# Weights and tables loaded inside the layer norms of a two-block network, not in stages of their own

## Chip, core and metric

One NeuronCore of one Trainium2 chip. The metric is the device time of one execution in microseconds, the median of the runs; every other time here comes from one profiled execution.

## What is computed

The input x is (4, 1024, 128) in float32: T = 4096 tokens of 128 channels. Two blocks follow one another, each of the form `x = x + s * silu(g)` with `xn = layernorm(x)`, where s is an attention of xn and g a small network of xn:

```python
xn = _layernorm(x); s = _L0_attn_ref(xn, ...)          # tiled softmax attention
g = _silu(_L0_ffn_ref(xn, ...))                        # layernorm*w+b, convolution, rotary causal attention,
x = x + s * g                                          #   layernorm*w+b, mixture of 4 experts
xn = _layernorm(x); s = _L1_attn_ref(xn, ...)          # causal attention, 16 heads
g = _silu(_L1_ffn_ref(xn, ...))                        # 6 layers: shift, local attention, shift,
x = x + s * g                                          #   layernorm*g+b, gated network
```

`_layernorm` is `(x - mean) / sqrt(var + 1e-5)` over the 128 channels, in some places followed by a weight and a bias.

## The kernel before

Activations lie transposed in SBUF, 128 channels on the partitions and 4096 tokens along the free dimension, 16 KB a partition: `x`, `s` and `cur` live through the whole program. The work is cut into stages (class `Stage`, L53), each a block of hand-written programs for the five engines with semaphores between them. At the end of a stage all engines meet in a barrier that also clears the stage's semaphores (the helper behind it has line L65 in the profile), and the next stage reuses them. Nothing of a stage starts before all engines are through with the one before. Inside a stage each engine runs its instructions in the order in which they are written.

`build_program` (L1518) writes the stages one after the other: load; ln0 (x to cur); tile attention in a loop over the 4 batches; load; ln1; convolution; the projections ci0; causal attention; load; ln2; router; experts; load; ln3; ci1; causal attention; load; and a loop over the 6 layers with shift1, local attention, shift2, ln4 and the gated network; then the end stage, which stores the output in 8 pieces. The change deals with the first four of the five load stages.

Of the kernel before, what the change touches and what calls it, by code (L numbers as in the profile page):

```python
# [105 lines left out]
def load_constants(nc, pairs):  # L106

    with Stage(nc, "load") as st:
        loaded = st.sem("loaded")
        with nc.Block() as block:  # L110

            @block.sync
            def _(sp):
                for dst, src in pairs:
                    sp.dma_start(dst, src).then_inc(loaded, 16)  # L115
                sp.wait_ge(loaded, 16 * len(pairs))

def layernorm(nc, name, ps, k, src, dst, weight=None, bias=None, fetches=()):  # L119

    with Stage(nc, name) as st:
# [6 lines left out]
        with nc.Block() as block:  # L130
# [27 lines left out]
            @block.scalar  # L158
            def _(act):
                for c in range(NCH):  # L160
                    act.wait_ge(centred, c + 1)
                    if c >= 4:
                        act.wait_ge(var_part, c - 3)
                    nc.scalar.activation(square[:, c % 4, :], dst[:, chunk(c)], ACT.Square).then_inc(squared, 1)  # L164
                act.wait_ge(var_eps, 1)
                nc.scalar.activation(rstd[:, :], rstd[:, :], ACT.Sqrt).then_inc(rooted, 1)  # L166
                if weight is not None:
                    for c in range(NCH):
                        act.wait_ge(scaled, c + 1)
                        nc.scalar.activation(dst[:, chunk(c)], dst[:, chunk(c)], ACT.Identity,  # L170
                                             bias=bias, scale=weight).then_inc(done, 1)
                    act.wait_ge(done, NCH)
# [1345 lines left out]
def build_program(nc, a, out):  # L1518

    with ExitStack() as whole:
# [12 lines left out]
        with ExitStack() as before:  # L1534
            k = dict(k, **buffers(before, CAUSAL))
            with ExitStack() as ctx:
                w = buffers(ctx, [n for n in a if n.startswith("ta_") and n != "ta_bv"])
                w["ta_bv"] = ctx.enter_context(nc.sbuf_tensor("sb_ta_bv", [P, P], F32))
                load_constants(nc, loads(k) + [(x[:, :], a["x"])] +
                               [(t[:], a[n].to_broadcast([P, P]) if n == "ta_bv" else a[n]) for n, t in w.items()])  # L1540
                layernorm(nc, "ln0", ps, k, x, cur)
                tile_attention(nc, ps, k, w, cur, s)

            with ExitStack() as ctx:
                vtok = ctx.enter_context(nc.sbuf_tensor("vtok0", [P, NT, P], F32))
                stacks, zeros = causal_stacks(nc, ctx, "ca0")
                w = buffers(ctx, ["cq", "ck", "cv", "cqs", "cks", "cproj", "taps", "ln1"])
                with ExitStack() as inner:
                    h, mixed = (inner.enter_context(nc.sbuf_tensor(n, [P, T], F32)) for n in ("h0", "h_mixed"))  # L1550
                    tables = buffers(inner, ["cos", "sin"])
                    load_constants(nc, loads(w) + loads(tables))
                    layernorm(nc, "ln1", ps, k, cur, h, w["ln1"][:, 0:1], w["ln1"][:, 1:2])
                    causal_convolution(nc, w["taps"], h, mixed)
                    causal_inputs(nc, "ci0", ps, mixed, dict(q=w["cq"], k=w["ck"], v=w["cv"], q_swapped=w["cqs"],
                                                             k_swapped=w["cks"]), tables, q_parts, k_parts, vtok, stacks, zeros)
                causal_attention(nc, "ca0", ps, k, q_parts, k_parts, vtok, stacks, zeros, w["cproj"], cur, cur)
            with ExitStack() as ctx:
                h = ctx.enter_context(nc.sbuf_tensor("h1", [P, T], F32))
                mask = ctx.enter_context(nc.sbuf_tensor("mask", [P, NT, E], BF16))  # L1560
                w = buffers(ctx, ["wv", "wp", "router", "ln2"])
                load_constants(nc, loads(w))
                layernorm(nc, "ln2", ps, k, cur, h, w["ln2"][:, 0:1], w["ln2"][:, 1:2])
                route(nc, ps, w["router"], h, mask)
                experts(nc, ps, k, w["wv"], w["wp"], h, mask, cur, s, x)

            with ExitStack() as ctx:
                vtok = ctx.enter_context(nc.sbuf_tensor("vtok1", [P, NT, P], F32))
                stacks, zeros = causal_stacks(nc, ctx, "ca1")  # L1570
                w = buffers(ctx, ["dq", "dk", "dv", "dproj"])
                load_constants(nc, loads(w))
                layernorm(nc, "ln3", ps, k, x, cur)
                causal_inputs(nc, "ci1", ps, cur, dict(q=w["dq"], k=w["dk"], v=w["dv"]), None, q_parts, k_parts, vtok, stacks, zeros)
                causal_attention(nc, "ca1", ps, k, q_parts, k_parts, vtok, stacks, zeros, w["dproj"], s, None)

# [152 lines left out]
```

## Time and profile before

| | us |
|---|---|
| median of 3 runs | 5986.9 (5984.35 to 5988.27) |
| the profiled execution | 5988.87 |
| its span in the trace | 5987.1 |
| PE busy | 4994.9 (83%) |
| DVE busy | 3999.0 (67%) |
| ACT busy | 3194.9 (53%) |
| POOL busy | 1770.2 (30%) |

The mean granted TensorE clock is 0.939 of full. A matmul, activation or vector instruction is told with the instant at which it starts, how long it ran, and in brackets how long its engine was idle before it and what released it; `SPq` rows are SP issuing a DMA. "PEq L65" as a releaser is the barrier between stages.

### The profile page before, as it was taken

The page shows a single profiled execution, that of the slowest core. Times are in us where ns is not written, and L with a number is a line of the kernel's source. Part 1 is how long each engine was busy: PE and PEld are TensorE (multiplying, and loading weights), DVE is VectorE, ACT ScalarE, POOL GpSimd, SP SyncE. Part 2 cuts the span into 40 slices and gives each one's busy share as a digit, 9 for nine tenths or more (in the row PEclk, how much of TensorE's full clock was granted, in tenths as well). Part 3 has the DMA queues.
Part 4 walks back from the last instruction along what each step waited for, and adds up shares of the span by engine and source line. Part 5 has one row for each costly group of instructions (what it writes and reads, how often), then busy time and mean ns, then how long its engine had stood idle before and what let it go on. Part 6 is the DMA issues. An engine that isn't in the chain of part 4 may idle for free. (4 is left out here: it accounts for less than half of the span.)

```text
span 5987.1 us, 168239 instructions
## 1 busy us (share of the span) xinstructions
PE 4994.9 (83%) x74422; PEld 2903.2 (48%) x74640; DVE 3999.0 (67%) x4814; ACT 3194.9 (53%) x3632; POOL 1770.2 (30%) x1242
## 2 busy tenths in 40 slices
PE   6757888688678877998899889987999799979997
PEld 3432333343333334665466546663666366636663
DVE  5767775332477756886688658865887488848884
ACT  2324556122245554775477546763776377636773
POOL 0020000000200004552355325542555155505550
PEclk9988999899889998999999999998999899989998
DMA  0011000000110001111111101110111111101111
GB/s 25 0 48 34 27 25 13 21 0 0 50 29 23 23 13 53 38 38 41 27 37 39 45 22 35 38 52 16 38 38 34 33 38 38 38 30 38 38 38 40
DMA packets 90446, 187.28 MB, mean 31 GB/s; under 512 B 26112, under 2 KB 42368, under 8 KB 87552
## 3 DMA queue, kind: packets, MB, share of 16 engines
q1 hardware_dynamic: 89728, 176.58, 11.3%
q8 instruction: 588, 9.63, 0.7%
q14 instruction: 130, 1.06, 0.1%
HBM read 60.10 MB, written 14.68 MB: 12 GB/s over the span
## 5 line engine op out<-in xcount | busy, mean ns | idle before, releaser
L1413 POOL TENSOR_TENSOR part_of_local<-part_of_local,sine_of_local 128x512 f32<-128x512 f32 x768 | 960.9, 1273 | 1060.7 <-DVE sine_of_local L1350 1060.7
L820 ACT ACTIVATE prob_of_ca<-ps 128x1024 f32<-128x1024 f32 (+3 forms) x768 | 600.0, 812 | 414.3 <-PE ps L667 254.7
L1420 POOL TENSOR_TENSOR part_of_local<-part_of_local,inverse_of_local 128x1024 f32<-128x1024 f32 x384 | 722.6, 1903 | 142.9 <-DVE inverse_of_local L1382 142.9
L685 PE MATMUL ps<-keys_of_ca,queries_of_ca 64*128 64x512 bf16 (+3 forms) x1536 | 329.5, 350 | 244.0 <-DVE top_of_ca L858 97.8
L1387 DVE TENSOR_REDUCE total_of_local<-prob_of_local 128x16 f32<-128x1024 f32 x192 | 234.3, 1220 | 417.0 <-ACT prob_of_local L1326 417.0
L1347 DVE TENSOR_TENSOR part_of_local<-ps,rope 128x1024 f32<-128x1024 f32 x384 | 466.4, 1215 | 45.0 <-ACT square_of_local L1294 45.0
L1186 PE MATMUL ps<-qkv,shifted 128*128 128x512 f32 x768 | 395.9, 639 | 88.9 <-POOL values_of_local L1423 77.5
L1350 DVE TENSOR_TENSOR sine_of_local<-ps,rope 128x1024 f32<-128x1024 f32 x384 | 465.9, 1213 | 0.0
L1196 PE MATMUL ps<-qkv,shifted 128*128 128x512 f32 x768 | 381.6, 619 | 82.6 <-ACT heads_out_of_local L1322 68.8
L1272 PEld LDWEIGHTS ps<-prob_t_of_local,mixed_of_local 64*64 64x64 f32 x12288 | 338.3, 134 | 165.0 <-issue 154.9
L858 DVE TENSOR_REDUCE top_of_ca<-ps 128x2 f32<-128x1024 f32 (+1 forms) x320 | 356.6, 1114 | 82.0 <-PE ps L667 64.5
L1281 PE MATMUL ps<-heads_out_of_local,wo 128*128 128x128 f32 x3072 | 392.5, 283 | 14.3 <-ACT heads_out_of_local L1322 14.1
L1272 PE MATMUL ps<-prob_t_of_local,mixed_of_local 64*64 64x32 f32 x12288 | 386.0, 220 | 14.8 <-issue 7.9
L1272 PE MATMUL ps<-prob_t_of_local,values_of_local 64*64 64x32 f32 x12288 | 381.9, 219 | 0.8 <-issue 0.2
L1281 PEld LDWEIGHTS ps<-heads_out_of_local,wo 128*128 128x128 f32 x3072 | 374.5, 199 | 16.4 <-ACT heads_out_of_local L1322 16.4
L1253 PE MATMUL ps<-qkv,shifted 128*64 128x512 f32 x1536 | 372.9, 606 | 0.0
L1312 ACT ACTIVATE keys_of_local<-ps 128x1024 f32<-128x1024 f32 x192 | 196.8, 1025 | 324.7 <-PE ps L1215 324.7
L1333 ACT ACTIVATE values_of_local<-ps 128x1024 f32<-128x1024 f32 x192 | 196.6, 1024 | 302.9 <-PE ps L1253 302.9
L1272 PEld LDWEIGHTS ps<-prob_t_of_local,values_of_local 64*64 64x64 f32 x12288 | 339.0, 135 | 2.5 <-issue 1.9
L759 PE MATMUL ps<-prob_of_ca,values_of_ca 128*32 128x512 f32 (+3 forms) x3072 | 335.8, 510 | 0.6 <-ACT summed_of_ca L806 0.4
L852 DVE TENSOR_REDUCE top_of_ca<-ps 128x1 f32<-128x512 f32 x384 | 262.9, 685 | 97.2 <-PE ps L685 96.8
L636 POOL COPY values_of_ca<-vtok 128x256 f32<-128x256 f32 x32 | 12.8, 402 | 1035.2 <-PE ps L759 1035.1
(206 smaller groups left out, 10169.1 us busy)
## 6 DMA issues: line engine op xcount, KB each, us to landing
mixed_of_local<-values_of_local SPq DMA_DIRECT2D x636, 128.0 KB
mixed_of_local<-values_of_local SPq DMA_DIRECT2D x264, 64.0 KB
queries_of_ca<-q_parts SPq DMA_DIRECT2D x384, 32.0 KB
keys_of_ca<-k_parts SPq DMA_DIRECT2D x384, 32.0 KB
qkv<-in_qkv SPq DMA_DIRECT2D x7, 1536.0 KB, 6.6
rope<-in_rope SPq DMA_DIRECT2D x7, 1024.0 KB, 9.1
q_parts<-parts_of_ci SPq DMA_DIRECT2D x16, 384.0 KB, 2.5
k_parts<-parts_of_ci SPq DMA_DIRECT2D x16, 384.0 KB, 2.5
```

What stands on the lines that cost most here:

```text
L759: last = nc.tensor.matmul(ps[h * QUAD:(h + 1) * QUAD, SUM_BANK, j:], values[:, G % 2, kt, h, :], prob[:, i % 2, h, j:], start=kt == 0, sto ...
L820: nc.scalar.activation(prob[:, i % 2, 2 * two:2 * two + 2, j:], ps[:, 2 * two:2 * two + 2, j:], ACT.Exp, scale=scale).then_inc(raised, 1)
L858: nc.vector.reduce_max(to, pair[:, :, 0:width], AX_X).then_inc(pair_used, 1)
L1186: last = nc.tensor.matmul(two_banks(SCORE_SLOT)[:, a, :], xs[:, tokens(t)], w["qkv"][:, 0, chunk(a)], start=True, stop=True)
L1196: last = nc.tensor.matmul(two_banks(KEY_SLOT)[:, a, :], xs[:, tokens(t)], w["qkv"][:, 1, chunk(a)], start=True, stop=True)
L1253: last = nc.tensor.matmul(two_banks(VALUE_SLOT)[h * DH:(h + 1) * DH, a, :], xs[:, t * P + a * DH:t * P + (a + 1) * DH], w["qkv"][:, 2, chu ...
L1272: last = nc.tensor.matmul(out, src[rows, t % RING * 2 + i // 2, p + e, :], prob_t[rows, p + e, i * WIN:(i + 1) * WIN], start=True, stop=True)
L1281: last = nc.tensor.matmul(two_banks(OUT_SLOT)[:, 0, 0:P], w["o"][:, p, :], heads_out[:, p, :], start=p == 0, stop=p == PAIRS - 1)
L1347: nc.vector.tensor_tensor(part[:, t % 2, side], by_head(slot), table(2 * side, t), ALU.mult).then_inc(parts, 1)
L1350: nc.vector.tensor_tensor(sine[:, side], by_head(slot), table(2 * side + 1, t), ALU.mult).then_inc(parts, 1)
L1413: nc.gpsimd.tensor_tensor(out, out, sine[:, side, :, (1 - to) * half:(2 - to) * half], ALU.add).then_inc(rotated, 1)
L1420: nc.gpsimd.tensor_tensor(part[:, t % 2, side], part[:, t % 2, side], by, ALU.mult).then_inc(scaled, 1)
```

## The change

1. The three `load_constants` ahead of ln1, ln2 and ln3 are dropped, and their loads become `fetches` of these layer norms. The fifth load stage stays.
2. The first load stage loads only x, now in 8 pieces of 512 tokens and ahead of the others, and the three constants that a layer norm uses (`mean`, `mean_row`, `pick_row`). The other constants and the weights of tile attention are `fetches` of ln0.
3. A flag `late_weight`, set for ln1 and ln2, whose own weight and bias (`w["ln1"]`, `w["ln2"]`) are among the fetches: ACT waits for all fetches after the root and before the first scaling.

```diff
-def layernorm(nc, name, ps, k, src, dst, weight=None, bias=None, fetches=()):
+def layernorm(nc, name, ps, k, src, dst, weight=None, bias=None, fetches=(), late_weight=False):
...
                 nc.scalar.activation(rstd[:, :], rstd[:, :], ACT.Sqrt).then_inc(rooted, 1)
+                if late_weight:
+                    act.wait_ge(fetched, 16 * len(fetches))
                 if weight is not None:
...
-                load_constants(nc, loads(k) + [(x[:, :], a["x"])] +
-                               [(t[:], a[n].to_broadcast([P, P]) if n == "ta_bv" else a[n]) for n, t in w.items()])
-                layernorm(nc, "ln0", ps, k, x, cur)
+                first = {n: k[n] for n in ("mean", "mean_row", "pick_row")}
+                load_constants(nc, [(x[:, chunk(c)], a["x"][:, chunk(c)]) for c in range(NCH)] + loads(first))
+                layernorm(nc, "ln0", ps, k, x, cur, fetches=loads({n: t for n, t in k.items() if n not in first}) +
+                          [(t[:], a[n].to_broadcast([P, P]) if n == "ta_bv" else a[n]) for n, t in w.items()])
...
-                    load_constants(nc, loads(w) + loads(tables))
-                    layernorm(nc, "ln1", ps, k, cur, h, w["ln1"][:, 0:1], w["ln1"][:, 1:2])
+                    layernorm(nc, "ln1", ps, k, cur, h, w["ln1"][:, 0:1], w["ln1"][:, 1:2], loads(w) + loads(tables), True)
...
-                load_constants(nc, loads(w))
-                layernorm(nc, "ln2", ps, k, cur, h, w["ln2"][:, 0:1], w["ln2"][:, 1:2])
+                layernorm(nc, "ln2", ps, k, cur, h, w["ln2"][:, 0:1], w["ln2"][:, 1:2], loads(w), True)
...
-                load_constants(nc, loads(w))
-                layernorm(nc, "ln3", ps, k, x, cur)
+                layernorm(nc, "ln3", ps, k, x, cur, fetches=loads(w))
```

The order of instructions shows what this does to SP's queue. At the start of the program (L115 is the load stage, the names are buffer and DRAM tensor), the difference on SP:

```order
 L112 UNCONDITIONAL_BRANCH
-L115 DMA sb_ident<-in_ident 128x128
-L115 DMA sb_ident_b<-in_ident_b 128x128
+L115 DMA x<-in_x 128x512 x8
 L115 DMA sb_mean<-in_mean 128x128
 L115 DMA sb_mean_row<-in_mean_row 128x64
 L115 DMA sb_pick_row<-in_pick_row 128x1024
```

The eight pieces of x have moved ahead of the constants, and the two identities have left the stage (as have, below these rows, the other 16 loads; x stood among them in one piece).

On SP around ln1, before, the end of the load stage and what follows it (L132 is SP's part of the layer norm, L499 that of ci0):

```order
L115 DMA sb_cks<-in_cks 128x128
L115 DMA sb_cproj<-in_cproj 128x512
L115 DMA sb_taps<-in_taps 128x3
L115 DMA sb_ln<-in_ln 128x2
L115 DMA sb_cos<-in_cos 128x1024
L115 DMA sb_sin<-in_sin 128x1024
L110 UNCONDITIONAL_BRANCH
L132 UNCONDITIONAL_BRANCH
L499 UNCONDITIONAL_BRANCH
L505 DMA q_parts<-parts_of_ci 128x3x512
```

and after the change, from the end of the loop over batches:

```order
L199 COMPARE_AND_BRANCH
L132 UNCONDITIONAL_BRANCH
L135 DMA sb_cq<-in_cq 128x128
L135 DMA sb_ck<-in_ck 128x128
L135 DMA sb_cv<-in_cv 128x128
L135 DMA sb_cqs<-in_cqs 128x128
L135 DMA sb_cks<-in_cks 128x128
L135 DMA sb_cproj<-in_cproj 128x512
L135 DMA sb_taps<-in_taps 128x3
L135 DMA sb_ln<-in_ln 128x2
L135 DMA sb_cos<-in_cos 128x1024
L135 DMA sb_sin<-in_sin 128x1024
```

The same ten loads in the same order, now behind the entry to the layer norm (L132) and not ahead of it.

## Rows read from the trace of the kernel before

**Rows 1.** The page: span, and busy time of each engine

```profile
span 5987.1 us, 168239 instructions
PE 4994.9 (83%) x74422; PEld 2903.2 (48%) x74640; DVE 3999.0 (67%) x4814; ACT 3194.9 (53%) x3632; POOL 1770.2 (30%) x1242
```

**Rows 2.** Timeline, first loading: start us, us, engine, line, operation, out<-in, count [idle before]

```profile
0.76 0.40 SPq L115 DMA_DIRECT2D sb_ident<-in_ident  x1
...
6.42 0.43 SPq L115 DMA_DIRECT2D x<-in_x  x1
...
11.03 0.53 SPq L115 DMA_DIRECT2D sb_ta_bv<-in_ta_bv  x1
...
17.98 8.72 PE L144 MATMUL ps<-x,sb_mean 128*128 128x512 f32 x16 [17.98 <-PEq L65]
```

**Rows 3.** Timeline, second loading and ln1

```profile
332.60 0.34 SPq L115 DMA_DIRECT2D sb_cq<-in_cq  x1
...
342.88 10.10 PE L144 MATMUL ps<-cur,sb_mean 128*128 128x512 f32 x16 [12.15 <-PEq L65]
...
370.19 0.69 DVE L188 TENSOR_TENSOR h<-h,ps 128x512 f32<-128x512 f32 x1 [0.17 <-PE ps L155]
371.05 0.69 DVE L188 TENSOR_TENSOR h<-h,ps 128x512 f32<-128x512 f32 x1 [0.17 <-PE ps L155]
```

**Rows 4.** Timeline, third and fourth loading, with ln2 and the start of ln3

```profile
1078.16 0.69 DVE L905 TENSOR_TENSOR cur<-ps,cur 128x512 f32<-128x512 f32 x1 [3.91 <-PE ps L723]
1079.98 0.38 SPq L115 DMA_DIRECT2D sb_wv<-in_wv  x1
...
1091.58 9.52 PE L144 MATMUL ps<-cur,sb_mean 128*128 128x512 f32 x16 [13.45 <-PEq L65]
...
1106.22 0.63 ACT L166 ACTIVATE rstd_of_ln<-rstd_of_ln 128x512 f32<-128x512 f32 x1 [0.56 <-DVE rstd_of_ln L181]
...
1113.12 0.81 ACT L170 ACTIVATE h<-h,sb_ln 128x512 f32<-128x512 f32 x1 [6.27 <-DVE h L188]
...
1546.36 0.33 SPq L115 DMA_DIRECT2D sb_dq<-in_dq  x1
...
1551.11 10.15 PE L144 MATMUL ps<-x,sb_mean 128*128 128x512 f32 x16 [8.94 <-PEq L65]
```

**Rows 5.** Timeline, ln4 of the first layer, which has loads beside it

```profile
2796.96 10.15 PE L144 MATMUL ps<-shifted,sb_mean 128*128 128x512 f32 x16 [5.94 <-PEq L65]
2797.07 0.35 SPq L135 DMA_DIRECT2D qkv<-in_qkv  x1
...
2825.18 0.69 DVE L188 TENSOR_TENSOR normed<-normed,ps 128x512 f32<-128x512 f32 x1 [0.17 <-PE ps L155]
```

**Rows 6.** Stretches: us, busy share of each engine, granted clock, DMA share, GB/s

```profile
2797.00:2808.00 11.00, 11.00 (x24) 4.13 (x24) 5.51 (x8) 2.52 (x4) 0.00 (x0) 0.72 0.77 292
2.00:3.00 1.00, 0.00 (x0) 0.00 (x0) 0.00 (x0) 0.00 (x0) 0.00 (x0) 1.00 0.42 96
...
332.00:333.00 1.00, 0.00 (x0) 0.00 (x0) 0.00 (x0) 0.00 (x0) 0.00 (x0) 0.50 0.00 0
...
1082.00:1083.00 1.00, 0.00 (x0) 0.00 (x0) 0.00 (x0) 0.00 (x0) 0.00 (x0) 0.89 0.76 295
1084.00:1085.00 1.00, 0.00 (x0) 0.00 (x0) 0.00 (x0) 0.00 (x0) 0.00 (x0) 0.50 0.99 426
5977.00:5978.00 1.00, 0.00 (x0) 0.00 (x0) 1.00 (x2) 0.10 (x1) 0.00 (x0) 0.50 0.70 262
```

**Rows 7.** Timeline, ACT's part of the second shift in layers 1, 2 and 3

```profile
2792.47 3.62 ACT L1071 ACTIVATE shifted<-cur 64x4096 f32<-64x4096 f32 x1 [5.28 <-PEq L65]
...
3405.93 3.62 ACT L1071 ACTIVATE shifted<-cur 64x4096 f32<-64x4096 f32 x1 [3.55 <-PEq L65]
...
4023.48 3.62 ACT L1071 ACTIVATE shifted<-cur 64x4096 f32<-64x4096 f32 x1 [5.06 <-PEq L65]
```

**Rows 8.** DMA issues: out<-in, count, KB each, median us from issue to landing

```profile
sb_spread_total<-in_spread_total SPq DMA_DIRECT2D x1, 256.0 KB, 2.7
```

## Prediction, made before the changed kernel ran

> **What bounds the kernel now.** I read the page first: TensorE is busy 83% of a span of 5987.1 us and VectorE 67% [rows 1]. That average is made in the attention parts and says nothing about the places that the change touches. So I went to the timeline around each of the four loading stages. In each of them every compute engine stands still: the columns of PE, DVE and ACT are zero while the DMA columns are not [rows 6]. A loading stage is an island: the stage before has ended, SP issues loads, waits for the last to land, and only then does a barrier let the layer norm begin. Its whole length is on the path that sets the end, whatever the average says.
>
> The four lengths are read as follows. In the first, SP issues 21 loads from 0.76 us, x being the 13th at 6.42 and the last at 11.03; the first matmul of the layer norm starts at 17.98 [rows 2]. In the second, PE's last matmul ended at 330.73 (342.88 less the 12.15 of idle in its row), SP issues from 332.60, and the layer norm starts at 342.88 [rows 3]. In the third, VectorE's last sum starts at 1078.16, SP issues from 1079.98, the layer norm starts at 1091.58 [rows 4]. In the fourth SP issues from 1546.36 and the layer norm starts at 1551.11 [rows 4].
>
> The kernel also has the form that the change wants: in the loop of six layers, layer norm ln4 starts its matmuls at 2796.96 and SP issues its first load at 2797.07, with no stage between [rows 5]. Over the 11 us from 2797 the DMAs move 292 GB/s, and the engines work beside them [rows 6].
>
> **The change part by part.**
>
> *The three dropped stages (ln1, ln2, ln3).* Without the stage, the barrier behind the work before opens on the layer norm itself. SP then issues its first load at the time at which it does now, and by ln4 the first matmul starts 0.11 us before SP's first load [rows 5]. So PE starts at 332.49, 1079.87 and 1546.25 where it started at 342.88, 1091.58 and 1551.11: gains of 10.39, 11.71 and 4.86 us, **26.96 us** together. SP issues the same 10, 4 and 4 loads; they only stand in another stage, and nothing else is on SP's queue until the first store of parts, one stage or two later. What hides them is the layer norm. Its length without any load beside it: in ln1, from 342.88 to the last multiplication, which starts at 371.05, 28.17 us [rows 3]. With 3.1 MB of loads beside it, in ln4, from 2796.96 to 2825.18: 28.22 us [rows 5]. The cost of the loads to the engines is 0.05 us, which I take as nothing.
>
> *The two added waits.* ACT now waits for all loads after the square root and before the eight scalings. Behind it on ACT stand only those eight, and what waits for them is the barrier. In ln2, where most is loaded, the square root starts 14.64 us after the first matmul (1106.22 less 1091.58) and the first scaling 21.54 us after it (1113.12) [rows 4]. The loads took 11.6 us from the first issue to PE's start, barrier and all. So the wait is over before ACT comes to it, with 3 us to spare, and some 10 us before the first scaling could run anyway. Cost: 0. If the cover were gone, each microsecond by which the loads land after 21.5 us would be a microsecond on the path. ln0 and ln3 have no scaling and get no such wait; there the barrier at the stage's end, some 29 us in, is what needs the loads, and 17 loads at the spacing of SP's issues ((11.03 − 0.76)/20 = 0.51 us) are issued in under 9 us.
>
> *The first load.* Before: 3.64 MB in 21 loads. After: x in eight pieces of 256 KB, and mean, mean_row and pick_row (64, 32 and 512 KB), 2.72 MB in 11 loads. x is first and so no longer waits for 12 others. From the third stage: 11.60 us from the first issue to PE's start, for 3.15 MB at the 426 GB/s of its middle [rows 6], which is 7.4 us; the remaining 4.2 us are start, landing and barrier. In the fourth, 4.75 us for 0.46 MB leave 3.5 us in the same way. The pieces of x have rows of 2 KB instead of 16 KB. Their rate I take from the store of the output, which has the same shape: 262 GB/s while the DMA engines were 0.70 busy, so 375 GB/s when full [rows 6]. Sum: 0.76 + 4.2 + 2.72/0.375 = 12.2 us in place of 17.98, a gain of **5.8 us**. The bounds: at 262 GB/s with no better filling PE starts at 15.3 (gain 2.6); at the 426 GB/s of wv with its rows of 16 KB [rows 6] and 3.5 us fixed it starts at 10.6 (gain 7.3). I take the value from the full rate because eight pieces are in flight at once.
>
> The Trainium skill, "DMA: Bandwidth & Descriptors", section on measured bandwidth, speaks against cutting x: it wants DMAs of 1 MiB or more and fits one DMA as 2.0 us plus its bytes over 436 GB/s, so 2.6 us for a 256 KB piece; eight one after the other would be 20.8 us, an estimate from the page. The rows speak for overlap, as the next part works out.
>
> *TensorE's clock.* The granted clock falls to 0.50, the lower of its levels (1.2 GHz), when PE has been idle: it is at 0.50 throughout 332 to 333, after the last matmul at 330.73, and it falls between 1082 and 1083, after one that ended at 1078.13 [rows 3, 4, 6]. Each of the three layer norms therefore starts at 0.50 now. At the full level (2.4 GHz) a chunk of two passes takes 0.86 us (371.05 less 370.19) [rows 3], so eight take some 7.1 us with the last one's end, while L144 takes 9.52 us in ln2 and 10.15 in ln3 [rows 4]. After the change ln2 starts 1.7 us after the last matmul, before the point where its clock fell; I count **2.4 us** there. For ln1 the new start (332.49) lies behind the fall and I count nothing; for ln3 the idle stretch is still 4 us and I count nothing. The bounds of this term are 0 and 2.4 + 3.1 + 3.1 = 8.6.
>
> *The sum.* 26.96 + 5.8 + 2.4 = 35.2 us. The profiled execution took 5988.87 us (span 5987.1), which becomes 5953.7 (span 5951.9). The median of the runs, 5986.9, is 2.0 below it; less 35.2 it is 5951.7, and I say **5952**.
>
> *What the rest of the program does with it.* Nothing else is reordered. But equal work does not take equal time here: from one layer's second shift to the next the first two distances are 613.46 and 617.55 us [rows 7], with the same instructions. A shift of everything by 35 us can deal these differences anew. I take 4 us, one such difference, to both sides; on the low side half of it, since the bounds there hold several gains at once.
>
> **The rivals.**
>
> *A. The clock stays up in all three layer norms.* For: the idle stretch before them shrinks to 1.7 to 4 us. Against: in ln1 the clock was down 1.3 us after the last matmul. Gain 26.96 + 5.8 + 8.6 = 41.4, so 5945.5 us.
>
> *B. The pieces of x do not overlap.* By the row of a 256 KB load with rows of 2 KB, one lands after 2.7 us [rows 8]; eight in turn are 21.6 us, and with the start of 0.76, the other three loads (1.6 us at 375 GB/s) and 1.1 us of barrier (from the end of VectorE's last work, 1078.85, to SP's first load in the third stage [rows 4]) PE starts at 25.1, 7.1 us later than now. Then 26.96 + 2.4 − 7.1 = 22.3 and 5964.6 us. This is what the skill's rule of size (cited above) would do here. Against it: SP issues at 0.5 us spacing, and in the first stage many loads were under way together.
>
> *C. The loads and the layer norm do not overlap after all.* If the engines were held up by as much as they gain, the three stages would give nothing and only ln0's 5.8 us stay: 5986.9 − 5.8 = 5981.1 us. For it: nothing but that ln4 is in a loop, and these are not. Against: ln4's 28.22 us beside 28.17. With ln0's bounds C reaches from 5979.6 to 5984.3; only if part of the overlap is kept does it fall below 5975, 12 us under the time before.
>
> *D. Slower: the loads starve beside running engines, and the ACT wait and the barriers sit on them.* Place: ln2's wait for wv and wp, 3.15 MB. Price: the time by which they land after the layer norm would be over (some 29 us), and as much less in the others. It decides from the point where this exceeds 35.2 + 12 = 47 us, so 3.15 MB in 76 us, 41 GB/s. The lowest rates in the trace are those of the small loads at the start, 96 GB/s [rows 6]; even at that rate wv and wp take 33 us, 4 us too long. At 40 GB/s the time would be some 6000 us. Against it stand ln4's 292 GB/s.
>
> *E. The change does not take effect.* It could be that the barrier holds the layer norm until SP is through with its issues. Order and rows say no: SP's loads stand behind the barrier in ln4 also, and PE started 0.11 us ahead of them. I give it no chance of its own beyond C.
>
> **How the numbers follow.** The forecast (with its bounds) has 0.80, A 0.10, B 0.04, C 0.04, D 0.02. A measurement of this kernel can tell about 0.2%, 12 us, from no change. Forecast, A and B are all faster by more than that (0.94), and a quarter of C, where part of the overlap is kept: 0.95. Same: the other 0.03 of C. Slower: 0.02 from D. The range: low 5986.9 − (26.96 + 7.3 + 8.6) = 5944.0, less half of the layers' 4 us, 5942; high 5986.9 − (26.96 + 2.6) = 5957.3, plus 4, 5961. It takes in A; B, C and D are left out.
>
> **What would show it.** In the profile after, the first matmul of L144 lies at some 12 us; in ln1 to ln3 PE starts within 0.3 us of SP's first load, and some 1.8 us after the last work before it; the layer norms are 28 us or less from first matmul to last multiplication; ACT's first scaling is released by DVE and not by a DMA; and ln2's L144 has a granted clock of 1.00 from the start. The prediction is wrong if the first matmul comes after 15.3 us, if a layer norm is longer than 29 us, if a scaling waits for a load, or if the time between the layer norms moves by more than 4 us in total.

## The result, and the profile after

The changed kernel takes 5939.87 us in the median of six runs (5932.0 to 5945.31), beside 5986.89 for the kernel before in six runs of its own: a ratio of 0.992, with a 95% interval of 0.9907 to 0.9933. Forecast were 5952 and a range of 5942 to 5961. The direction and the mechanism are as forecast; the gain is 47.0 us where 35.2 were counted, and the time lies 2 us under the range.

The profiled execution has a span of 5938.9 us, 48.2 less than before. Its page, against [rows 1] (PEclk is the granted clock in 40 slices of the span, in tenths):

```profile
span 5938.9 us, 168180 instructions
...
PE 4971.1 (84%) x74422; PEld 2888.7 (49%) x74640; DVE 4000.0 (67%) x4814; ACT 3197.4 (54%) x3632; POOL 1770.4 (30%) x1242
...
PEclk9988999899799998999999999999999899989999
```

PE does the same 74422 matmuls and is busy 23.8 us less. DVE and ACT are busy as long as before. Only a higher clock makes the same matmuls shorter; its mean went from 0.939 to 0.947. That is the first sign that something beside the dropped waits has changed.

The timeline at the start and at the three layer norms, against [rows 2] to [rows 4]:

```profile
0.75 3.73 SPq L115 DMA_DIRECT2D x<-in_x  x8
...
5.64 0.43 SPq L115 DMA_DIRECT2D sb_pick_row<-in_pick_row  x1
...
12.23 9.76 PE L144 MATMUL ps<-x,sb_mean 128*128 128x512 f32 x16 [12.23 <-PEq L65]
...
320.06 0.33 SPq L135 DMA_DIRECT2D sb_cq<-in_cq  x1
320.22 8.82 PE L144 MATMUL ps<-cur,sb_mean 128*128 128x512 f32 x16 [2.03 <-PEq L65]
...
1056.32 0.69 DVE L907 TENSOR_TENSOR cur<-ps,cur 128x512 f32<-128x512 f32 x1 [5.61 <-PE ps L725]
1058.13 0.38 SPq L135 DMA_DIRECT2D sb_wv<-in_wv  x1
1058.17 8.80 PE L144 MATMUL ps<-cur,sb_mean 128*128 128x512 f32 x16 [1.89 <-PEq L65]
...
1072.10 0.63 ACT L166 ACTIVATE rstd_of_ln<-rstd_of_ln 128x512 f32<-128x512 f32 x1 [0.56 <-DVE rstd_of_ln L183]
...
1079.06 0.82 ACT L172 ACTIVATE h<-h,sb_ln 128x512 f32<-128x512 f32 x1 [6.34 <-DVE h L190]
...
1512.00 0.33 SPq L135 DMA_DIRECT2D sb_dq<-in_dq  x1
1512.16 8.82 PE L144 MATMUL ps<-x,sb_mean 128*128 128x512 f32 x16 [4.35 <-PEq L65]
```

The first matmul starts at 12.23 us, where 12.2 was worked out. In ln1 to ln3 PE now starts beside SP's first load: 0.16, 0.04 and 0.16 us after it, not 0.11 ahead. And the row of L172, the first scaling of ln2, still has DVE as its releaser: the added wait for the loads costs nothing.

Where the 48.2 us of the two traces came from, each the difference of the same instants in both:

| place | before | after | gain |
|---|---|---|---|
| to the first matmul | 17.98 | 12.23 | 5.75 |
| from the end of the last work to ln1 | 11.33 | 1.21 | 10.12 |
| the same, ln2 | 12.72 | 1.16 | 11.56 |
| the same, ln3 | 5.83 | 1.24 | 4.59 |
| ln0 to ln3, first matmul to end of the last multiplication, together | 114.55 | 110.71 | 3.84 |
| tile attention | 284.92 | 278.27 | 6.65 |
| convolution, ci0, first causal attention | 707.12 | 709.20 | -2.08 |
| router and experts | 425.55 | 425.44 | 0.11 |
| end of ln3 to first matmul of ln4 | 1216.96 | 1219.61 | -2.65 |
| from there to the end of the span | 3190.10 | 3179.80 | 10.30 |

The first four rows, 32.0 us, are what the change does by its code; forecast were 26.96 + 5.8 = 32.8. The fifth is the clock in the layer norms, forecast as 2.4. The last five rows hold 12.3 us in places whose instructions the change does not touch. The experiments are about these. One pair of traces does not fix the first rows to the tenth of a microsecond: before PE's first matmul stand 17.2 to 18.3 us in seven traces with the first load of before and 12.2 to 12.9 in eight with that of the change, and the gap ahead of ln1 was 10.5 to 11.5 with its loading stage. In the mean of all traces the first five rows come to 34.6 us instead of 35.9.

### The profile page after: what moved, and what is told of

The parts are those of the page before. It is cut to its first block and busy times, and to the rows that moved or that the text cites. A ratio compares the mean times of both kernels' runs of the same rounds, so it can differ in the third digit from the quotient of the medians.

```text
span 5938.9 us, 168180 instructions
## 1 busy us (share of the span) xinstructions
PE 4971.1 (84%) x74422; PEld 2888.7 (49%) x74640; DVE 4000.0 (67%) x4814; ACT 3197.4 (54%) x3632; POOL 1770.4 (30%) x1242
## 5 line engine op out<-in xcount | busy, mean ns | idle before, releaser
L1283 PEld LDWEIGHTS ps<-heads_out_of_local,wo 128*128 128x128 f32 x3072 | 367.9, 196 | 17.2 <-ACT heads_out_of_local L1324 17.2
```

Source lines behind the costliest of these rows:

```text
L1283: last = nc.tensor.matmul(two_banks(OUT_SLOT)[:, 0, 0:P], w["o"][:, p, :], heads_out[:, p, :], start=p == 0, stop=p == PAIRS - 1)
```

## The experiments

**Theory 1:** the change is worth its start, its gaps and its shorter layer norms, some 36 us; the 12 us are chance, because every part of the program falls anew against the rises and falls of TensorE's clock. **Theory 2:** the surplus belongs to the change; the idle stretches that it drops keep the clock up elsewhere too. **Theory 3** came later and is told there.

In the table, "difference" is the mean of the kernel's runs less the mean of the kernel before in runs on the same chip, with its standard error; "fixed" is what the kernel should differ by from its start, gaps, pauses and layer norms alone.

| kernel | runs | median us | ratio, 95% interval | difference | fixed |
|---|---|---|---|---|---|
| changed kernel | 6 | 5939.87 | 0.9920 (0.9907 to 0.9933) | -47.8 ± 2.2 | -35.8 |
| after_again (the same) | 6 | 5940.59 | 0.9932 (0.9919 to 0.9945) | -42.3 ± 3.4 | -35.8 |
| drop_three | 4 | 5950.04 | 0.9942 (0.9925 to 0.9958) | -33.2 ± 3.2 | -30 |
| first_only | 10 | 5983.44 | 1.0003 (0.9994 to 1.0013) | +3.2 ± 2.3 | -5.8 |
| before_pause | 10 | 5988.15 | 1.0010 (1.0001 to 1.0020) | +6.8 ± 2.6 | +3.6 |
| after_pause | 4 | 5944.00 | 0.9932 (0.9916 to 0.9949) | -38.6 ± 1.9 | -32.2 |
| only_ln3 | 5 | 5967.74 | 0.9967 (0.9954 to 0.9980) | -18.7 ± 2.4 | -6.1 |
| undo_ln3 | 5 | 5944.83 | 0.9927 (0.9913 to 0.9941) | -43.4 ± 3.0 | -29.7 |
| gap1_ln3 | 5 | 5947.77 | 0.9935 (0.9922 to 0.9948) | -39.1 ± 2.3 | -32.9 |
| gap3_ln3 | 6 | 5941.03 | 0.9923 (0.9910 to 0.9936) | -46.9 ± 3.3 | -32.4 |
| before_gap1 | 11 | 5982.62 | 1.0002 (0.9992 to 1.0011) | +1.0 ± 2.2 | +0.3 |
| before_gap2 | 12 | 5981.11 | 1.0000 (0.9990 to 1.0010) | -2.1 ± 2.9 | +2.2 |
| pieces | 6 | 5936.73 | 0.9928 (0.9913 to 0.9944) | -44.9 ± 4.2 | -42.8 |
| before_warm | 5 | 5930.22 | 0.9922 (0.9908 to 0.9935) | -46.0 ± 2.7 | |
| after_warm | 4 | 5896.68 | 0.9865 (0.9846 to 0.9883) | -81.0 ± 4.2 | |
| pieces_warm | 4 | 5892.97 | 0.9863 (0.9848 to 0.9877) | -87.4 ± 4.4 | |

### The two halves of the change, and a pause

`drop_three` keeps the first load of before and drops the three stages; `first_only` is the other half. `before_pause` and `after_pause` put a stage ahead of ln0 that only takes time:

```diff
+def pause(nc, n):
+    with Stage(nc, "pause") as st:
+        idle, chain = st.sb("idle", [P, CH]), st.sem("chain")
...
+                for _ in range(n):
+                    link(nc.vector.memset(idle[:, :], 0.0))
...
+                pause(nc, 4)
                 layernorm(nc, "ln0", ps, k, x, cur)
```

> The kernel before with only the three loading stages ahead of ln1, ln2 and ln3 dropped; the first load as before. Both theories: ln1, ln2 and ln3 begin 10.4, 11.7 and 4.9 us sooner after the work before them, 27 us. Theory 1 (the surplus of the change over the forecast is chance: every part of the program falls anew against the changes of TensorE's clock): the rest, from tile attention to the end, moves by any amount up to some 10 us either way, tile attention itself not more than a few us since its start is that of before; 5950 to 5968. Theory 2 (the dropped idle stretches keep the clock up, so the surplus of 12 us belongs to this part): the mean granted clock is 0.945 or more and the time 5945 to 5952.

> The kernel before with only the first load changed (x in eight pieces first, the rest beside ln0). Both theories: the first matmul at 12.2 us, a gain of 5.8. Theory 1 (chance of the clock): tile attention gains as in the changed kernel (6 to 7 us beside the 5.8) or not, the rest moves by up to 10 us either way; 5970 to 5990. Theory 2 (the surplus belongs to the dropped stages): 5981, within 2 us, and the mean clock stays at 0.939.

> The kernel before with a stage of its own ahead of ln0 in which VectorE alone works some 2 us (four writes of 128x512 in a chain, and a barrier): nothing in the program changes but that everything after it starts 3 to 4 us later. Theory 1 (chance of the clock): the time does not move by just that; 5980 to 6000, and the mean clock differs from 0.939 by 0.002 or more. Theory 2: 5990, within 2 us of the length of the pause, the mean clock 0.939.

> The changed kernel with the same pause of 3 to 4 us ahead of ln0. Theory 1: 5930 to 5955, by any amount other than the pause, with a mean clock that differs from 0.946 by up to 0.004. Theory 2: 5943 to 5944, the 5939.9 of the changed kernel and the pause.

Measured: 5950.04, 5983.44, 5988.15 and 5944.00 us. The start and the gaps read in the traces are near what both theories had: the first matmul of drop_three at 17.44, that of first_only at 12.86 (12.2 expected), and in drop_three 1.21, 1.16 and 1.24 us from the last work to ln1, ln2 and ln3. As to the times, Theory 2 did the better in three of the four: drop_three's 5950.04 is within its 5945 to 5952 (and at the very edge of Theory 1's), and the pauses of 3.6 us moved the medians by 5.3 and 4.1, where Theory 1 had them jump. Both lie within Theory 1's wide ranges too, so this is weak evidence. first_only's 5983.44 lies within Theory 1's 5970 to 5990 and just outside Theory 2's 5979 to 5983. Its mechanism, a clock kept up by less idle time, wanted a mean clock of 0.945 in drop_three; the trace has 0.944, and the one run differs from the next by as much. What these runs don't bear out is Theory 1 in the form that a shift deals each kernel a new time. The dealing goes on from one execution of a kernel to the next.

The surprise is the kernel before. In these runs it went from 5972.78 to 5989.42 us, over 19 runs, where the three runs shown ahead of the prediction spanned 3.9 us. Over all 79 of its runs in this study the mean is 5982.4, the standard deviation of one 6.4, and they go from 5969.3 to 5999.4; the six that the result was compared with, three of them those ahead of the prediction, were the quietest set, with a standard deviation of 1.7 (5.0 to 6.7 in the five others). In the 29 runs of first_only and the kernel before together, time and mean clock of an execution correlate at -0.88. So an execution of unchanged code wanders by 6 us with the clock, and a single trace of each kernel cannot say where 12 us come from.

What no fixed part explains is first_only, 9 us worse than its own with a standard error of 2.3. I return to that at the end.

### The program cut to the places of the change

`short_before` and `short_after` leave out both causal attentions, the six layers and the load ahead of them:

```diff
-                causal_attention(nc, "ca0", ps, k, q_parts, k_parts, vtok, stacks, zeros, w["cproj"], cur, cur)
...
-                causal_attention(nc, "ca1", ps, k, q_parts, k_parts, vtok, stacks, zeros, w["dproj"], s, None)
...
-            with nc.Fori(0, LAYERS) as layer:
...
         gate_and_store(nc, ps, x, s, cur, out)
```

> The kernel before cut down to what surrounds the four loading stages: both causal attentions and the six layers are left out, so nothing of them is computed; some 1150 us. It serves as the base of short_after, with less than a fifth of the program exposed to the changes of the clock, so that its runs should lie within 4 us of each other.

> The changed kernel cut down in the same way. Theory 1 (the change is worth what the five places show in the two traces: 5.75 us at the start, 10.1 + 11.6 + 4.6 in the gaps ahead of ln1 to ln3, 3.7 in the shorter layer norms, 35.7 in all; the rest is the clock's chance in the other parts): 34 to 38 us under short_before. Theory 2 (a further 9 us belong to the change itself, in tile attention, router and experts behind the layer norms): 42 us or more under it.

Measured: medians of 1058.82 us (1055.94 to 1061.82, four runs) and 1029.91 (1029.28 to 1030.48, four runs), 28.9 us apart (29.0 ± 1.5 in the means). That is less than either theory said, and the runs of short_before spread over 5.9 us where I had 4. The traces tell why: the first matmul moved from 17.22 to 12.66 (4.6 us), the gaps shrank by 9.5, 10.5 and 4.8, 29.4 in all, and the four layer norms together by 2.3, ln1 by nothing. The sum of 31.7 is 3 above the measured difference. My 3.7 for the layer norms was one execution's value and not a constant. But 42 us is far off: in this program the layer norms' neighbours (tile attention, router, experts) hold no surplus. If there is one, it lies in the parts that are left out here, or needs them.

### x in one piece

`x_whole` issues x as one DMA ahead of the three constants:

```diff
-load_constants(nc, [(x[:, chunk(c)], a["x"][:, chunk(c)]) for c in range(NCH)] + loads(first))
+load_constants(nc, [(x[:, :], a["x"])] + loads(first))
```

> The changed kernel with x loaded by one DMA instead of eight, still ahead of the three constants. Theory 1 (the pieces overlap, the row length of 2 KB costs little): the first matmul between 11.2 and 12.5 us, where the changed kernel has 12.23. Rival (pieces of 256 KB cost bandwidth, as the rule of size has it): at 10.4 or sooner, so the cutting cost 2 us.

One run, 5947.72 us, which says little of a microsecond; its trace says more. With x in eight pieces the first matmul starts at 12.15 and 12.23 in two traces of the changed kernel and at up to 12.86 in the six others that load x so ahead of ln0:

```profile
0.75 0.40 SPq L115 DMA_DIRECT2D x<-in_x  x1
...
11.17 1.19 PE L144 MATMUL ps<-x,sb_mean 128*128 128x512 f32 x1 [11.17 <-PEq L65]
```

The cutting costs 1.0 to 1.7 us by this one trace. The start lies 0.03 us below the first expectation and 0.8 above the second: the pieces overlap, as the rows said. The Trainium skill's rule of size ("DMA: Bandwidth & Descriptors", section on measured bandwidth), which asks for DMAs of 1 MiB or more, holds here in its direction, at this small price. Loading x in one piece would buy that time back, unless something uses the pieces as they come (`pieces`, below).

> The changed kernel itself, for the spread of its executions and a second trace. Theory 1: the median comes nearer to the forecast than the first six runs did, 5940 to 5950, the runs spread over 10 us or more, and the surplus in the trace stands in other stages than in the first one. Theory 2: 5938 to 5941, with tile attention again 6 us shorter than before (308 us from the first matmul of ln0 to that of ln1).

The edit is none. The median was 5940.59, within what both theories said; the runs went from 5932.65 to 5946.83. In the trace Theory 2's place for the surplus is gone. Tile attention: 326.96 - 1.21 - 12.15 - 28.68 = 284.9 us, which is what it took before. In its place ln2 was shorter:

```profile
1063.93 7.11 PE L144 MATMUL ps<-cur,sb_mean 128*128 128x512 f32 x16 [1.89 <-PEq L65]
```

7.11 us is the full clock throughout; in the first trace the same sixteen matmuls after the same idle of 1.89 us took 8.80. But the total came out at 5940 again, so the surplus as such did not go away, and Theory 1 does not say why.

### How ln3 meets the clock

Comparing all traces, I found that L144 of ln0, ln1 and ln2 differs from execution to execution, but that of ln3 does not. It took 9.98 to 10.15 us in every trace with the loading stage and 8.82 in every one without. It looks as if the experts' stage ahead of it lined the program up with the clock's changes; no run takes that stage away, so this stays an inference. And from the first matmul of ln3 to that of ln4, a stretch with the same instructions everywhere but for four loads, the traces with a long L144 took longer:

| traces | L144 of ln3 | ln3 to ln4, us |
|---|---|---|
| before, first_only, before_pause | 10.15, 10.07, 10.01 | 1245.9, 1251.4, 1251.9 |
| changed, after_again, after_pause, drop_three, x_whole | 8.82 in all | 1246.9, 1239.6, 1240.0, 1246.8, 1243.5 |

**Theory 3:** this is systematic: which way ln3 meets the clock is set by the distance from the experts' stage, and the rest of the program keeps something of it. Four kernels set that distance. `only_ln3` drops the stage ahead of ln3 alone; `undo_ln3` puts it back into the changed kernel; `gap1_ln3` and `gap3_ln3` put pauses of one and three writes ahead of ln3 there and move no load.

```diff
-                load_constants(nc, loads(w))
-                layernorm(nc, "ln3", ps, k, x, cur)
+                layernorm(nc, "ln3", ps, k, x, cur, fetches=loads(w))
```

```diff
+                pause(nc, 1)
                 layernorm(nc, "ln3", ps, k, x, cur, fetches=loads(w))
```

> The kernel before with the loading stage ahead of ln3 alone dropped. Both theories: the gap ahead of ln3 4.6 us shorter, the layer norm 1.5 us shorter, 6.1 us. Theory 3 (the experts' stage lines the program up with the changes of TensorE's clock, so that ln3 always meets the clock in one way with the loading stage and in another without it, and the rest of the program keeps something of that): L144 of ln3 takes 8.8 us as in every trace of the changed program, and the time is 10 to 18 us under that before. Theory 1 (chance): 4 to 8 us under it.

> The changed kernel with the loading stage ahead of ln3 put back. Theory 3: L144 of ln3 takes 10.0 to 10.2 us as in every trace of the program before, and the time is 10 to 18 us over that of the changed kernel, so 5950 to 5958. Theory 1: 4 to 8 us over it, 5944 to 5948.

> The changed kernel with a pause ahead of ln3 (one write of 128x512 by VectorE and a barrier, some 1.6 us), no load moved. Theory 3: ln3 meets the clock as before the change, L144 takes 10 us, and the time is 6 to 12 us over that of the changed kernel, several times the pause. Theory 1: 1.6 us over it, within 3 us.

> The changed kernel with a longer pause ahead of ln3 (three writes, some 2.9 us). Theory 3: ln3 meets the clock between the two ways; L144 takes 8.9 to 9.5 us, and the time is less than with the shorter pause or within 2 us of it, although the pause is longer. Theory 1: 2.9 us over the changed kernel, within 3 us, and 1.3 over the shorter pause.

The two first matmuls of the stretch in undo_ln3, then in gap1_ln3, then in only_ln3:

```profile
1522.27 10.04 PE L144 MATMUL ps<-x,sb_mean 128*128 128x512 f32 x16 [9.15 <-PEq L65]
...
2770.01 9.11 PE L144 MATMUL ps<-shifted,sb_mean 128*128 128x512 f32 x16 [5.93 <-PEq L65]
```

```profile
1517.65 10.00 PE L144 MATMUL ps<-x,sb_mean 128*128 128x512 f32 x16 [5.79 <-PEq L65]
...
2766.39 8.57 PE L144 MATMUL ps<-shifted,sb_mean 128*128 128x512 f32 x16 [5.93 <-PEq L65]
```

```profile
1549.75 8.82 PE L144 MATMUL ps<-x,sb_mean 128*128 128x512 f32 x16 [4.38 <-PEq L65]
...
2792.05 9.08 PE L144 MATMUL ps<-shifted,sb_mean 128*128 128x512 f32 x16 [5.94 <-PEq L65]
```

L144 of ln3 came out as set in all four (10.04, 10.00, 8.82, and 9.33 in gap3_ln3). It is not the idle before it that decides: gap1_ln3's 5.79 us of idle gives 10.00, and gap3_ln3's 7.14 gives 9.33. The stretch to ln4 took 1247.7 and 1248.7 us in the two long ones and 1242.3 and 1242.6 in the others. So far Theory 3.

The times do not follow as neatly. only_ln3 gained 18.7 us, where Theory 1 had 4 to 8; gap1_ln3 lies 7.9 over the changed kernel's median with a pause of some 1.5; gap3_ln3 lies 1.2 over it although its pause is longer. These three look like Theory 3. undo_ln3 should have been 10 to 18 us over the changed kernel by it, and was 5.0. That is Theory 1's number. But these medians come from different sets of runs. By the column "difference", each against before on its own chip, gap1_ln3, gap3_ln3 and undo_ln3 lie 5.9 over, 1.9 under and 1.6 over the -45.0 of the changed kernel (the mean of its two comparisons), each with an error of some 3: they decide little, and only only_ln3 stands out.

So the same was set in the kernel before, where no load moves, by a pause ahead of its fourth loading stage:

> The kernel before with a pause of some 2.1 us ahead of its fourth loading stage (two writes by VectorE and a barrier), no load moved. Theory 3 (how ln3 meets the clock is fixed by the distance from the experts' stage, and the rest of the program keeps some 6 us of it): ln3 meets the clock as in the changed kernel, its L144 takes 8.8 us, and the time is 3 to 9 us under that before although the program is longer. Theory 1 (chance): L144 also 8.8 us, but the time is that before or up to 2 us over it.

> The same with a pause of 1.4 us (one write): ln3 meets the clock about as with the longer pause in the changed kernel, L144 9.3 us. Theory 3: 2 to 9 us under the time before. Theory 1: within 2 us of it.

```profile
1545.09 8.97 PE L144 MATMUL ps<-x,sb_mean 128*128 128x512 f32 x16 [11.27 <-PEq L65]
...
2786.92 9.28 PE L144 MATMUL ps<-shifted,sb_mean 128*128 128x512 f32 x16 [5.93 <-PEq L65]
```

This is before_gap2: the stretch took 1241.8 us; in before_gap1 it took 1240.1. But the times were -2.1 ± 2.9 and +1.0 ± 2.2 against before: the first between the two theories, the second Theory 1's number and outside what Theory 3 said. What holds over fifteen traces is the stretch alone: 1249.1 us in the mean of the five with an L144 of 10 us or more (1245.9 to 1251.9), 1242.6 in the ten others (1239.6 to 1246.9), 6.6 us apart, of which 1.2 are ln3 itself. What Theory 3 wanted beyond that stretch is not there: from ln4 to the end the five took 3181.2 us and the ten 3179.8. In the pair of traces shown with the result it is not even in the stretch: before took 1245.9 us there, with an L144 of 10.15, and the changed kernel 1246.9, with 8.82. And the whole times of the kernels scatter about their fixed parts plus such a stretch by more than their standard errors. Theory 3 is kept for the stretch and given up as an account of the whole surplus.

### The clock held up by fillers

If the surplus is the clock's, a program that gives the clock less occasion to fall should show the bare worth of the change. `keep_busy` gives PE 14 small matmuls into an unused bank, whose results nothing reads, where it waits for the reciprocal in a layer norm and in each shift stage. `before_warm`, `after_warm` and `pieces_warm` are the kernel before, the changed kernel and `pieces` with it; `pieces` drops the first loading stage too and lets PE wait for each load.

```diff
+def keep_busy(nc, ps, k, some, n):
+    for _ in range(n):
+        nc.tensor.matmul(ps[:, 5, 0:P], k["mean"][:, :], some[:, 0:P], start=True, stop=True)
...
+                keep_busy(nc, ps, k, src, 14)
                 pe.wait_ge(inverse, 1)
...
+            @block.tensor
+            def _(pe):
+                keep_busy(nc, ps, k, x, 14)
```

```diff
+                for (to, of), sem in zip(first, got):
+                    sp.dma_start(to, of).then_inc(sem, 16)
                 for to, of in fetches:
...
+                    if first:
+                        pe.wait_ge(got[1 + c], 16)
```

> The changed kernel without the first loading stage either: mean, the eight pieces of x, mean_row and pick_row are issued in ln0 in this order, and PE waits for each by itself. The first matmul starts at 3.5 to 4.5 us in place of 12.2; the matmuls of a chunk (1.7 us at the lower clock) are slower than a piece (0.7 us), so only the first wait counts. 6 to 9 us under the changed kernel, 5931 to 5935.

> The same, and PE is given 14 small matmuls into an unused bank while it would wait for the reciprocal in each layer norm and during each shift stage (18 and 12 places are idle for 4.8 and 5.9 us; nothing reads the results). If the clock's falls there are what costs, L144 takes 7.1 us and L155 7.1 us in place of 8.5 to 10.2, 1.5 to 3 us in each of the ten layer norms: 15 to 30 us under pieces. If the fillers come too late or push the real matmuls back, no gain or a loss of 1 us in each.

> The kernel before with 14 small matmuls for PE while it waits for the reciprocal in each layer norm and in each shift stage. L155 takes 7.1 us in all ten layer norms and L144 7.1 us in the six behind a shift; L144 stays near 10 us behind the loading stages. By pieces_warm less pieces 30 to 55 us under the time before.

> The changed kernel with the same fillers. Theory 1 (the change is worth its start, its gaps and the shorter L144 of three layer norms, the rest is chance): 33 to 37 us under before_warm. Theory 3 (more of the program gains by the way in which it meets the clock): 40 us or more under it. Against pieces_warm it should be some 7 us longer, the later first matmul.

The layer norm ln4 of the first layer in before_warm (L122 are the fillers, L150 and L162 what L144 and L155 were), against [rows 5]:

```profile
2790.32 3.36 PE L122 MATMUL ps<-cur,sb_mean 128*128 128x128 f32 x28 [1.56 <-PEq L65]
2794.80 7.10 PE L150 MATMUL ps<-shifted,sb_mean 128*128 128x512 f32 x16 [1.11 <-PEq L65]
...
2806.20 3.39 PE L122 MATMUL ps<-shifted,sb_mean 128*128 128x128 f32 x28
2811.10 7.13 PE L162 MATMUL ps<-rstd_of_ln,sb_pick_row 128*128 128x512 f32 x16 [1.51 <-DVE rstd_of_ln L190]
```

The matmuls of the mean take 7.10 us where they took 10.15, those of pick_row 7.13, and the whole layer norm 24.16 where it took 28.91. All six ln4 of all three warm traces have these numbers. The kernel before_warm takes 5930.22 us, 46.0 ± 2.7 under before. And after_warm is 35.0 us under before_warm in the means (4.0 of standard error), 33.5 in the medians: Theory 1's 33 to 37, though Theory 3's 40 is only 1.2 standard errors away. In their traces the start went from 17.34 to 12.31, the gaps from 11.49, 12.50 and 6.12 to 1.21, 1.16 and 1.30, and ln1 to ln3 shrank by 1.2, 0.6 and 1.2: 5.0 + 26.4 + 3.0 = 34.4. With the fillers in place the change is worth its fixed part, within that error.

pieces starts its first matmul at 5.22 us (I had 3.5 to 4.5) and its median is 3.1 under the changed kernel (I had 6 to 9), of 7.0 in the trace; with a spread of 5919.88 to 5948.32 it cannot be told from it. The fastest kernel of the study is pieces_warm, 5892.97, 87.4 ± 4.4 us under before on its chip; its lead over after_warm, 3.7 in the medians, is within the error. It lies 43.8 us under pieces in the medians, where I had 15 to 30: the fillers give more than the layer norms that I had counted.

## Why the prediction missed

**The three dropped stages: right.** Forecast 10.39, 11.71, 4.86; the trace 10.12, 11.56, 4.59. Each is 0.15 to 0.27 less, because PE started just behind SP's first load and not 0.11 us ahead as in ln4.

**The loads beside the layer norms, and the two added waits: right.** ln2 with 3.15 MB beside it is shorter than before, not longer, and the first scaling still waits for DVE. Rivals C and D fall with it. B, pieces that do not overlap, falls with 12.23 us; x_whole puts the price of cutting at 1.0 to 1.7.

**The first load: right,** 12.2 forecast, 12.23 and 12.15 measured. Two slips in its working change nothing: 4.75 us less 0.46 MB at 426 GB/s leaves 3.7 us and not 3.5, which puts the lower bound at 10.8; and the fit of 2.0 us plus bytes over 436 GB/s stands in the Trainium skill's "DMA: Bandwidth & Descriptors" under the anatomy of one DMA, for those issued through GpSimd, not under measured bandwidth.

**TensorE's clock: the mechanism was seen, the size was not.** I counted 2.4 us in ln2 and nothing in ln1 and ln3. Measured in the first pair of traces: 1.3, 0.8 and 1.6 us, 3.7 in all. The picture behind it was also wrong in detail. I took it that a layer norm which starts before the fall keeps the high clock. In the changed kernel's trace the clock falls just after PE has started again and rises soon:

```profile
1058.00:1059.00 1.00, 0.83 (x2) 0.60 (x3) 0.00 (x0) 0.00 (x0) 0.00 (x0) 0.82 0.00 0
1059.00:1060.00 1.00, 1.00 (x2) 0.37 (x2) 0.21 (x1) 0.00 (x0) 0.00 (x0) 0.50 1.13 246
...
1062.00:1063.00 1.00, 1.00 (x4) 0.43 (x3) 0.47 (x2) 0.63 (x1) 0.00 (x0) 0.97 0.97 410
...
1512.00:1513.00 1.00, 0.84 (x2) 0.55 (x3) 0.00 (x0) 0.00 (x0) 0.00 (x0) 0.81 0.02 6
1513.00:1514.00 1.00, 1.00 (x2) 0.41 (x2) 0.16 (x1) 0.00 (x0) 0.00 (x0) 0.50 0.46 132
```

(The granted clock is the third number from the right, 0.82, 0.50, 0.97 and so on.) Before, it had fallen during the loading stage and stayed low for longer behind the first matmul. The gain is the difference of two low stretches. ln3, for which I counted nothing after 4 us of idle, had the most.

**"What the rest of the program does with it": the step that failed.** I wrote that a shift "can deal these differences anew", put it at nothing in the sum, gave it 4 us to both sides, and then took only half of that below. The two traces differ by 12.3 us in places that the change does not touch. One of my own signs of being wrong came with that: tile attention alone, between ln0 and ln1, moved by 6.65 us, where 4 was the limit. Three things were wrong. The spread of the program was read from three runs, 3.9 us, while one execution has a standard deviation of 6.4. The differences between layers [rows 7], 4 us for one of six, were taken once and not for a whole program of such parts. And some 6.6 us from ln3 on are not chance: with the loading stage and no pause every trace met the clock there in the slow way, and without the stage and a pause none did. The mean of six runs on each side has a standard error of 3.7 us in the difference from this alone (6.4 times the root of 2/6), and a median has somewhat more. In hindsight the bounds needed some 6 us more on both sides: 5936 to 5967, which holds the result.

**What stays open.** The change measured -47.8 and -42.3 us in two comparisons, 45 or so, against 35.8 of fixed parts (34.6 by the mean of all traces). With an error of 2 to 2.5 us in that 45, chance alone is an unlikely account of the 9 us between. Of these, the stretch from ln3 to ln4 can account for some 5 by the two groups of traces, though not in the pair shown. But kernels that should show this stretch (before_gap1, undo_ln3) did not in their times, and first_only missed its fixed part by 9 us the other way. The table shows one more pattern: in all nine comparisons without fillers in which at least one of the three stages is dropped, the kernel lies below its fixed part, by 2 to 15 us (8.6 in the mean), and the four kernels that drop none lie between 4 below and 9 above. That speaks for a surplus that comes with the dropped stages, as Theory 2 had it, and not with every shift; but four of the nine share one set of runs of before, the one with the highest mean, and the smallest two are within their errors. In the fifteen traces it cannot be pinned to a place: between the nine kernels that drop two or three stages and the six that drop one or none, tile attention, convolution to causal attention, and router with experts differ by 0.2 to 0.7 us, and the stretch from ln4 to the end by 5.3 ± 2.7 (3183.4 and 3178.2). Each kernel also seems to have an offset of its own of several microseconds; the runs here can't tell it from their errors in every case. What sets it was not found; it may be how each meets the clock in other parts, or something else that changes with the program. The cut and the warm pair, in which the clock has less room, show no surplus over the fixed parts: 29.0 ± 1.5 against 31.7, and 35.0 ± 4.0 against 34.4.

## What to carry to other kernels

A stage that only loads is worth its whole length when all engines stand still in it, and can be taken out, here at no cost that the layer norms' lengths show, if the stage behind it has an idle DMA queue and does not use the data at once; read the gap from the end of the last work to the next first matmul, and put the barrier that stays against it. A gain that hangs on TensorE's clock should get bounds as wide as the program's own wander, which three runs did not show here and 79 did. And a few small matmuls where PE waits 4 to 6 us for other engines can be worth more than the loads: here 46 us against 45.

## What the runs showed of the hardware

The granted clock's fall depends on more than the length of the idle stretch: after 1.89 us of idle ahead of ln2 the same matmuls took 8.80 us in one execution and 7.11 in another, and ahead of ln3 an idle of 4.35 us gave 8.82, of 5.79 gave 10.00, of 7.14 gave 9.33 and of 9.15 gave 10.04. Behind the experts' stage it was the same in every trace: 8.82 in the ten without a loading stage or pause ahead of ln3, 9.98 to 10.15 in the six with the loading stage alone. The fillers kept the clock up through the waits that were 4.8 and 5.9 us long: L144 of ln4 took 7.10 or 7.11 us in all six layers of all three traces. The Trainium skill, "TensorE: Matmul & The Clock Gate", part 1, says that the point at which the clock rises varies with the moment at which the first matmul lands, and advises against fitting to a fixed count of slow matmuls. The traces agree: L144 of ln0 took 9.76 us in one trace of the changed kernel and 8.74 in another. They add that behind the experts' stage, where ln3 starts, it did not vary.

Eight loads of 256 KB with rows of 2 KB, issued 0.47 us apart, had ln0 start 1.0 to 1.7 us later than one load of 2 MB with rows of 16 KB did, which is one trace.
